# Weights of the node stages loaded one stage ahead, and the score weights of two layers made in the listing stage

## The chip, the cores and the metric

The kernel runs on 1 core of one Trainium2 chip. The metric is the device time of one execution in microseconds, the median of several runs.

## The reference

A graph with 3125 nodes of 256 features and 50000 edges passes through four parts, each followed by `x = layernorm(x + part(x))`. The first applies a long product of plane rotations. The second, with which this change has to do most, is a gated network of three attention layers:

```
x0 = x * gate(x, query);  h = concat(x0, query, x * query)
h = relu(rgat(h, W1, q1, k1, b1))            # 4 heads of 128
h = h + relu(rgat(h, W2, q2, k2, b2))        # 4 heads of 128
h = relu(rgat(h, W3, q3, k3, b3))            # 1 head of 128
out = h @ proj_w + proj_b + x0, divided by its norm

def rgat(x, W, Q, K, b):                     # per edge type r
    xw = einsum('ni,rio->rno', x, W)
    alpha = softmax over the edges into dst of leaky_relu(xw[type, dst] @ Q + xw[type, src] @ K)
    return segment_sum(xw[type, src] * alpha, dst) + b
```

The third part gathers `h1[src]` times a filter of the edge features (two small layers), sums by dst and applies two output layers `o1`, `o2`. The fourth gathers `x @ W + b` by dst, takes the mean by src and is added. Everything is float32.

## The kernel before

The program is written out in `build` (L3099) as a row of stages. Each is one block in which every engine has its own stream, with semaphores between them, and at its end all engines meet at a barrier (`Mem.__exit__`, L87). Nothing of a stage starts before that. The nodes are cut into 25 tiles of 125.

- `layer0_list` (L112), the listing stage, lists the rotations of the first part. VectorE ranks the edges and makes six planes; TensorE turns a row with the windows of the chunks (L347), then the planes (L353, 24 turnings, two PSUM banks in turn); ScalarE copies them out (L333); VectorE goes on when all six are copied (L265). SP loads six inputs at the start (L158, L160), which VectorE waits for (L171).
- `attention` (L1235), phases sum1, sum2, sum3, sums over the edges of a layer. 424 steps of 125 edges go in 36 blocks of T = 12 steps. GpSimd gathers a row per edge and step (L1299) into a ring of three blocks, and waits for TensorE's sums only when the ring is full. SP loads a mask for each block when the one three blocks back is used (L1322 to L1325). VectorE makes the scores of a block once its 12 gathers have landed (L1492), TensorE sums (L1412), VectorE adds to the table `agg`.
- `nodes_attend` (L2041), phases attend1 and attend2, makes the table of the next layer out of `agg`. VectorE divides and adds the bias (`attend`), TensorE turns the tile (`turn`, L2109), ScalarE copies it (`take_turned`), TensorE multiplies it by the next layer's weights W (`table`, L2122, L2125) and by the score weights (L2130), VectorE and ScalarE copy the results out and SP stores them. In attend2 ScalarE first folds the rows kept from layer 1 (L2172), three tiles ahead. GpSimd scatters two or three columns of the source list and one of the queries per tile (L1206, L1213).
- The score weights are products of W with the key and query vectors q and k. They let a node's scores come out of the same multiplication as its table row. `projection_load` (L1689) loads q, k, W and the transposed W at the start of the node stage, TensorE forms the products (`score_weights`, L1698: 4 blocks x 2 edge types x 4 or 1 matmuls) ahead of the first table, and VectorE copies them (L1711). The same helper serves the gate stage, where nothing changes.
- `nodes_mix` (L2243) and `nodes_filter` (L2728) are the node stages after sum3 and after the filter sum. Each loads its weights at its start on SP, then its x rows by groups of four tiles, one group after the other; TensorE and VectorE wait for all the weights (`landed`). In `nodes_mix` VectorE adds the projection bias to the x rows (`outer_bias`, L2422) before it squares the first group.
- `filter_sum` (L2490) sums the filtered messages in 106 quads of four steps; SP loads edge features and selections ahead (L2559, L2565).

Matmuls and turnings in float32 are recorded as two instructions each, so 32 matmuls show as 64. A stage's order on each engine is the order in which its function issues; nothing rearranges it.

## Time and profile before

| | us |
|---|---|
| median of 3 runs | 5727.86 |
| lowest and highest | 5724.3, 5733.14 |
| the profiled execution | 5721.64 |
| its span | 5719.8 |
| TensorE busy in it | 3820.1 (67%) |
| GpSimd busy | 3434.1 (60%) |
| VectorE busy | 2961.3 (52%) |
| ScalarE busy | 1971.7 (34%) |

The span runs from the first to the last recorded instruction. No engine is busy throughout: the stages have different limits, and a share over the whole span says little about one of them. The mean granted clock of TensorE is 0.772 of full speed; it has two levels, 1.2 and 2.4 GHz, shown as 0.50 and 1.00. In the rows PE is TensorE's matmuls, PEld its weight loads, DVE VectorE, ACT ScalarE, POOL GpSimd, SP the engine that issues most transfers; a q behind the name (SPq) marks the issue itself.

### The profile page before, as it was taken

To read this page: it belongs to the slowest core of one execution; us is meant where nothing else is said; L and a number is where in the kernel's file an instruction comes from. 1 tells how busy PE (TensorE), PEld (TensorE's weight loads), DVE (VectorE), ACT (ScalarE), POOL (GpSimd) and SP (SyncE) were. 2 spreads that over 40 slices of the span, in tenths; PEclk is the share of its full clock that TensorE was granted. 3 is DMA by queue.
4 is the path that set the end of the run, shared out by engine and by line. 5 is a ranking of instruction groups with operands and counts; after the bars stand their busy time and mean duration, and the time that the engine had idled before them with its cause. 6 is when DMAs were issued, how large, how long until landed. Compare 5 with 4: busy or idle time off the path is not lost. (4 is left out here: it accounts for less than half of the span.)

```text
span 5719.8 us, 76686 instructions
## 1 busy us (share of the span) xinstructions
PE 3820.1 (67%) x19501; PEld 2762.5 (48%) x19509; DVE 2961.3 (52%) x6738; ACT 1971.7 (34%) x4763; POOL 3434.1 (60%) x2759
## 2 busy tenths in 40 slices
PE   6599721795777769677776534444499998655553
PEld 6466510453555555355555433333367776433332
DVE  6666547422555542355554444444477887433334
ACT  0133200001666641266565112121089998200000
POOL 0122220377887735677773788885677776488884
PEclk6699955797888889788888755555799999766565
DMA  0000012234666633566663333332355554343332
GB/s 8 19 13 13 11 35 79 73 76 103 175 176 165 167 101 90 127 176 170 159 163 86 69 80 84 85 83 81 78 144 149 150 148 129 78 104 84 84 84 72
DMA packets 536302, 567.65 MB, mean 99 GB/s; under 512 B 327551, under 2 KB 419741, under 8 KB 535915
## 3 DMA queue, kind: packets, MB, share of 16 engines
q0 software_dynamic: 349600, 362.07, 26.4%
q1 hardware_dynamic: 183190, 196.56, 12.1%
q10 hardware_dynamic: 3250, 6.40, 0.4%
q14 instruction: 204, 1.67, 0.1%
q8 instruction: 58, 0.95, 0.1%
HBM read 469.70 MB, written 92.22 MB: 98 GB/s over the span
## 5 line engine op out<-in xcount | busy, mean ns | idle before, releaser
L1299 POOL DMA_INDIRECT sum_gx_sb<-scratch_xw,keep_k_row_step_sb x1272 | 1588.4, 1249 | 427.9 <-issue 355.2
L1412 PE MATMUL sum_a_ps<-sum_gx_sb,sum_sel_sb 125*125 125x258 f32 (+1 forms) x4320 | 1190.1, 438 | 459.5 <-ACT sum_gx_sb L1348 178.9
L1412 PEld LDWEIGHTS sum_a_ps<-sum_gx_sb,sum_sel_sb 125*125 125x125 f32 x4320 | 916.9, 238 | 647.4 <-issue 451.7
L1348 ACT ACTIVATE sum_gx_sb<-sum_gx_sb,sum_wt_sb 125x129 f32<-125x129 f32 x3312 | 981.8, 388 | 544.1 <-DVE sum_wt_sb L1541 544.1
L1206 POOL DMA_INDIRECT scratch_grouped<-keep_k_value_sb,keep_k_place_sb x400 | 481.1, 1203 | 252.6 <-issue 135.1
L2537 POOL DMA_INDIRECT filter_gx_sb<-scratch_h,keep_k_src_step_sb x424 | 529.0, 1248 | 170.7 <-issue 97.8
L3013 POOL DMA_INDIRECT source_gx_sb<-scratch_h,source_grouped_sb x424 | 526.6, 1242 | 140.2 <-issue 117.5
L3025 PE MATMUL source_s_ps<-source_gx_sb,source_sel_sb 125*125 125x257 f32 x848 | 371.1, 614 | 308.9 <-DMA source_gx_sb<-scratch_h,source_grouped_sb 308.9
L3025 PEld LDWEIGHTS source_s_ps<-source_gx_sb,source_sel_sb 125*125 125x125 f32 x848 | 246.8, 305 | 433.2 <-issue 172.4
L2599 PE MATMUL filter_ps<-filter_m_sb,filter_h_sb 128*125 128x256 f32 x1696 | 387.3, 381 | 8.0 <-DVE filter_h_sb L2669 7.4
L3053 DVE TENSOR_TENSOR keep_agg_sb<-source_s_ps,keep_agg_sb 125x257 f32 x424 | 181.1, 427 | 386.6 <-PE source_s_ps L3025 380.6
L2599 PEld LDWEIGHTS filter_ps<-filter_m_sb,filter_h_sb 128*125 128x125 f32 x1696 | 318.0, 188 | 64.9 <-DVE filter_h_sb L2669 17.2
L542 POOL TENSOR_TENSOR turn_lm_sb<-turn_lt_sb,turn_masks_sb 128x256 f32<-128x256 f32 x23 | 16.7, 725 | 551.8 <-DVEq L476 551.8
L1572 DVE TENSOR_TENSOR keep_agg_sb<-sum_a_ps,keep_agg_sb 125x516 f32 (+1 forms) x360 | 201.2, 559 | 150.4 <-PE sum_a_ps L1412 104.8
L3037 ACT ACTIVATE source_root_sb<-source_root_sb 125x25 f32<-125x25 f32 x1 | 0.2, 226 | 690.7 <-DVE source_root_sb L3089 690.7
L1548 DVE TENSOR_TENSOR sum_sel_sb<-sum_iota_sb,keep_k_dloc_sb 125x500 f32<-125x500 f32 x324 | 219.5, 678 | 36.2 <-issue 29.3
L2642 ACT ACTIVATE filter_lg_sb<-filter_lg_sb,filter_half_sb 128x1000 f32<-128x1000 f32 x212 | 230.0, 1131 | 7.4
L2639 ACT ACTIVATE filter_lg_sb<-filter_lg_sb 125x1024 f32<-125x1024 f32 (+1 forms) x212 | 210.6, 1040 | 7.3
L1341 ACT ACTIVATE sum_wexp_sb<-sum_dw_sb 48x126 f32<-48x126 f32 (+1 forms) x108 | 33.1, 307 | 499.7 <-DVEq L1531 499.6
L1580 DVE SCALAR_TENSOR_TENSOR keep_agg_sb<-keep_agg_sb,sum_fac_sb,sum_a_ps 125x129 f32 x324 | 93.5, 345 | 196.3 <-PE sum_a_ps L1412 189.1
L2675 DVE TENSOR_TENSOR filter_f_sb<-filter_ps,filter_mb_sb 125x1024 f32<-125x1024 f32 x106 | 129.8, 1225 | 123.8 <-PE filter_ps L2599 119.2
L2611 PE MATMUL filter_ps<-filter_ms_sb,filter_sel_sb 125*125 125x256 f32 x720 | 180.7, 394 | 6.2 <-issue 6.2
(520 smaller groups left out, 6342.3 us busy)
## 6 DMA issues: line engine op xcount, KB each, us to landing
scratch_hots<-sum_cuts_sb SPq DMA_DIRECT2D x108, 244.1 KB
filter_sel_sb<-scratch_hots SPq DMA_DIRECT2D x106, 244.1 KB
filter_ea_sb<-in_ea_t SPq DMA_DIRECT2D x848, 24.4 KB
sum_gx_sb<-scratch_xw,keep_k_row_step_sb POOLq DMA_INDIRECT x1272
scratch_xw<-gate_xsb_sb SPq DMA_DIRECT2D x50, 253.9 KB
scratch_xw<-attend_xsb_sb SPq DMA_DIRECT2D x25, 507.8 KB
filter_gx_sb<-scratch_h,keep_k_src_step_sb POOLq DMA_INDIRECT x424
source_gx_sb<-scratch_h,source_grouped_sb POOLq DMA_INDIRECT x424
```

The costliest lines, as they stand in the source:

```text
L1206: nc.gpsimd.indirect_dma_start(out=dr["grouped"], out_offset=bass.IndirectOffsetOnAxis(ap=keep["place"][:, t:t + 1], axis=0), in_=keep["va ...
L1299: nc.gpsimd.indirect_dma_start(out=gx[:, q, j, :], out_offset=None, in_=table, in_offset=bass.IndirectOffsetOnAxis(ap=keep["row_step"][:, ...
L1348: last = nc.scalar.activation(here, here, ACT.Copy, scale=wt[q][:, h, j:j + 1])
L1412: last = mm(psa[b][0:P, half, 0:BF], sel[:, 0, p, j, :], gx[:, q, at, half * BF:(half + 1) * BF], **flags)
L1548: vec.tensor_tensor(sel[:, 0, p], iota[0:P, 0:P].unsqueeze(1).broadcast_to([P, HF, P]), keep["dloc"][:, bass.ds(s * T + p * HF, HF)].unsqu ...
L1572: vec.tensor_tensor(here, psa[b][0:P, :, 0:BF], here, ALU.add).then_inc(added, steps)
L2537: nc.gpsimd.indirect_dma_start(out=gx[:, n % LAP, j, :], out_offset=None, in_=dr["h2"], in_offset=bass.IndirectOffsetOnAxis(ap=keep["src_s ...
L2599: last = mm(ps2[0:P, j, :], h1[r % 2][:, b, j * P:j * P + P], m2[:, b, :], start=(b == 0), stop=(b == 1))
L2639: nc.scalar.activation(lg[:], lg[:], ACT.Exp, scale=-1.0)
L2642: nc.scalar.activation(lg[:], lg[:], ACT.Ln, scale=0.5, bias=half[0:lg.shape[0], :]).then_inc(made, 1)
L3013: nc.gpsimd.indirect_dma_start(out=gx[:, h % RING, j, :], out_offset=None, in_=dr["h3"], in_offset=bass.IndirectOffsetOnAxis(ap=grouped[:, ...
L3025: nc.tensor.matmul(pss[q % 2][0:P, j, 0:W], sel[:, q % 2, j, :], gx[:, q, j, :], start=True, stop=True).then_inc(summed, 1)
```

## The change

- Layers 2 and 3: the score weights are made in the listing stage, from transposed weights and q, k vectors loaded there (2 x 1024 KB and 2 x 256 KB and the vectors) behind the stage's six first loads. TensorE makes them between the turning of the windows and that of the planes, ScalarE copies them (`keep_wk_sb`) after its two sines. They stay in SBUF.
- W of layers 2 and 3 is loaded during the sum stage before (`coming_w_sb`): SP's mask loop is cut in two, 3 rounds of 3 blocks, then the loads, then the rest. The six loads of `nodes_mix` go to the same place in sum3.
- The seven loads of `nodes_filter` are issued at the end of SP's laps in `filter_sum`.
- The four node stages no longer load weights, no longer wait for them, and form no score weights. The sum stages end only when the loads have landed.

The buffers of the weights live over two stages (`coming1` to `coming4`), which adds no barrier. The core of the diff:

```diff
+    psk = mem.ps("k")
+    later = [score_buffers(mem, 2, wk[0], 4, psk[:, 0:256]), score_buffers(mem, 3, wk[1], 1, psk[:, 256:512])]
...
+            for n, sc in zip((2, 3), later):
+                score_load(nc, sp, sc, dr[f"W{n}_t"], dr[f"L1_gnn_k{n}"], dr[f"L1_gnn_q{n}"], weights_in)
...
+            act.wait_ge(scores, 1)
+            for sc in later:
+                n = sc["blocks"] * 2 * 2 * sc["heads"]
+                nc.scalar.copy(sc["wk"][:].rearrange("p b r s -> p (b r s)"), sc["psk"][:, 0:n]).then_inc(scores_kept, 1)
+            act.wait_ge(scores_kept, 2)
...
             nc.tensor.transpose(psm[0:1, 8:8 + EP], first[:], ident[0:EP, 0:EP]).then_inc(win_made, 1)
+            pe.wait_ge(weights_in, 16 * 8)
+            for sc in later:
+                last = score_weights(nc, sc)
+            last.then_inc(scores, 1)
             pe.wait_ge(plane_made, 1)
...
-            with sp.Fori(0, NS // 3 - 1) as i:
+            def next_masks(i):
                 for q in range(3):
                     sp.wait_ge(mask_used, 3 * i + q + 1)
                     sp.dma_start(mk[:, q, :], dr["masks"][bass.ds(3 * i + q + 3, 1), 0:HT, :].rearrange(
                         "o p c -> p (o c)")).then_inc(m_in[q], 16)
                     if H == 1:
                         store_cuts(3 * i + q)
+
+            EARLY = 3
+            with sp.Fori(0, EARLY) as i:
+                next_masks(i)
+            if H == 4:
+                for r in range(2):
+                    sp.dma_start(coming[:, :, r, :], dr[f"L1_gnn_W{layer + 1}"][r].rearrange("(b p) o -> p b o", p=128)).then_inc(coming_in, 16)
+            else:
+                load_mix_weights(sp, dr, coming, coming_in)
+            with sp.Fori(EARLY, NS // 3 - 1) as i:
+                next_masks(i)
+            sp.wait_ge(coming_in, 16 * (2 if H == 4 else 6))
             if H == 1:
                 for s in range(NS - 3, NS):
...
+def score_buffers(mem, n, wk, heads, psk):
+
+    outs = {4: 4, 1: 1}[heads]
+    return dict(blocks=4, heads=heads, outs=outs, wk=wk, psk=psk, wt=mem.sb(f"wt{n}", [128, outs, 2, 512]),
+                qk=mem.sb(f"qk{n}", [128, outs, 2, heads]))
+
+
+def score_load(nc, sp, sc, wt, k, q, sem):
+    with nc.allow_non_contiguous_dma(reason="short rows of the key and query vectors"):
+        sp.dma_start(sc["qk"][:, :, 0, :], k.rearrange("(o p) h -> p o h", p=128)).then_inc(sem, 16)
+        sp.dma_start(sc["qk"][:, :, 1, :], q.rearrange("(o p) h -> p o h", p=128)).then_inc(sem, 16)
+    for r in range(2):
+        sp.dma_start(sc["wt"][:, :, r, :], wt[r].rearrange("(o p) b -> p o b", p=128)).then_inc(sem, 16)
 
...
-    pr = projection_buffers(mem, 4, F, H)
+    pr = dict(w=w, wk=wk, heads=H, width=F, psx=[mem.ps(f"x{r}") for r in range(2)], psk=mem.ps("k"))
...
-            projection_load(nc, sp, pr, *(dr[n] for n in names), weights_in)
...
-                if not t:
-                    pe.wait_ge(wk_made, 1)
...
-            pe.wait_ge(weights_in, 16 * PROJECTION_LOADS)
-            score_weights(nc, pr).then_inc(scores_made, 1)
...
-                    act.wait_ge(wk_made, 1)
...
-            dve.wait_ge(scores_made, 1)
-            take_score_weights(nc, pr)
-            dve.drain()
-            dve.nop().then_inc(wk_made, 1)
...
+def load_mix_weights(sp, dr, w, sem):
+    sp.dma_start(w["b3"][:], dr["L1_gnn_b3"].partition_broadcast(P)).then_inc(sem, 16)
+    sp.dma_start(w["ident"][:], dr["c_ident"]).then_inc(sem, 16)
+    sp.dma_start(w["pw"][:], dr["L1_gnn_proj_w"]).then_inc(sem, 16)
+    for n, name in (("pb", "L1_gnn_proj_b"), ("ab", "L2_gnn_aw_b")):
+        sp.dma_start(w[n][:], dr[name].partition_broadcast(P)).then_inc(sem, 16)
+    sp.dma_start(w["aw"][:], dr["L2_gnn_aw_W"].rearrange("(b p) o -> p b o", p=128)).then_inc(sem, 16)
+
...
-            sp.dma_start(b3[:], dr["L1_gnn_b3"].partition_broadcast(P)).then_inc(landed, 16)
-            sp.dma_start(ident[:], dr["c_ident"]).then_inc(landed, 16)
-            sp.dma_start(pw[:], dr["L1_gnn_proj_w"]).then_inc(landed, 16)
-            for t, name in ((pb, "L1_gnn_proj_b"), (ab, "L2_gnn_aw_b")):
-                sp.dma_start(t[:], dr[name].partition_broadcast(P)).then_inc(landed, 16)
-            sp.dma_start(aw[:], dr["L2_gnn_aw_W"].rearrange("(b p) o -> p b o", p=128)).then_inc(landed, 16)
...
-            pe.wait_ge(landed, 16 * 6)
...
-            dve.wait_ge(landed, 16 * 6)
...
+def load_filtered_weights(nc, sp, dr, w, sem):
+    with nc.allow_non_contiguous_dma(reason="a short vector"):
+        sp.dma_start(w["b1"][:], dr["L2_gnn_o1_b"].rearrange("(b p) -> p b", p=128)).then_inc(sem, 16)
+    sp.dma_start(w["ident"][:], dr["c_ident"]).then_inc(sem, 16)
+    for n, name in (("w1", "L2_gnn_o1_W"), ("w2", "L2_gnn_o2_W"), ("w3", "L3_gnn_W")):
+        sp.dma_start(w[n][:], dr[name].rearrange("(b p) o -> p b o", p=128)).then_inc(sem, 16)
+    for n, name in (("b2", "L2_gnn_o2_b"), ("b3", "L3_gnn_b")):
+        sp.dma_start(w[n][:], dr[name].partition_broadcast(P)).then_inc(sem, 16)
...
             laps(sp, lap)
+            load_filtered_weights(nc, sp, dr, coming, coming_in)
+            sp.wait_ge(coming_in, 16 * 7)
...
-            pe.wait_ge(landed, 16 * 7)
...
-            act.wait_ge(landed, 16 * 7)
...
-            dve.wait_ge(landed, 16 * 7)
...
+        for n, width, heads in ((1, 512, 4), (2, 128, 1)):
+            with phase(f"coming{n}") as held:
+                w = held.sb("w", [128, 4, 2, width])
+                with phase(f"sum{n}") as mem:
+                    attention(nc, mem, dr, keep, agg, 4, 512, n, w)
+                with phase(f"attend{n}") as mem:
+                    nodes_attend(nc, mem, dr, keep, agg, f"L1_gnn_b{n}", w, wk[n - 1], width, heads, n == 1)
+        with phase("coming3") as held:
+            weights = mix_weights(held)
+            with phase("sum3") as mem:
+                attention(nc, mem, dr, keep, agg, 1, 128, 3, weights)
+            with phase("mix") as mem:
+                nodes_mix(nc, mem, dr, keep, agg, weights)
+        with phase("coming4") as held:
+            weights = filtered_weights(held)
+            with phase("filter") as mem:
+                filter_sum(nc, mem, dr, keep, agg, weights)
+            with phase("filtered") as mem:
+                nodes_filter(nc, mem, dr, keep, agg, weights)
```

TensorE in the listing stage, from its first matmuls on. `listed_m_ps` gets the small products and the turned windows (the third row), `listed_t_ps` the planes. Before:

```order
L344 MATMUL listed_m_ps<-listed_rank_sb,listed_tri_sb 125x1
L345 MATMUL listed_m_ps<-listed_rank_sb,listed_ones_sb 125x1
L347 MATMUL listed_m_ps<-listed_ident_sb,listed_first_sb 1x125
L353 MATMUL listed_t_ps<-listed_ident_sb,listed_planes_sb 100x125 x24
L364 MATMUL listed_c_ps<-listed_valued_sb,listed_picked_sb 64x32 x500
```

and now:

```order
L354 MATMUL listed_m_ps<-listed_rank_sb,listed_tri_sb 125x1
L355 MATMUL listed_m_ps<-listed_rank_sb,listed_ones_sb 125x1
L357 MATMUL listed_m_ps<-listed_ident_sb,listed_first_sb 1x125
L1747 MATMUL listed_k_ps<-listed_qk_sb,listed_wt_sb 128x8 x32
L1747 MATMUL listed_k_ps<-listed_qk_sb,listed_wt_sb 128x2 x8
L367 MATMUL listed_t_ps<-listed_ident_sb,listed_planes_sb 100x125 x24
```

Forty score matmuls (`listed_k_ps`) stand ahead of the planes.

TensorE at the head of attend1, from the turning of tiles 0 and 1 on (`attend_t_ps`); `attend_x_ps` is the table, `attend_k_ps` the scores. Before:

```order
L2109 MATMUL attend_t_ps<-attend_ident_sb,attend_raw_sb 128x125 x8
L1705 MATMUL attend_k_ps<-attend_qk_sb,attend_wt_sb 128x8 x32
L2122 MATMUL attend_x_ps<-attend_w_sb,attend_ht_sb 125x512 x8
L2130 MATMUL attend_k_ps<-attend_wk_sb,attend_ht_sb 125x16 x4
L2109 MATMUL attend_t_ps<-attend_ident_sb,attend_raw_sb 128x125 x4
```

and now:

```order
L2150 MATMUL attend_t_ps<-attend_ident_sb,attend_raw_sb 128x125 x8
L2163 MATMUL attend_x_ps<-coming_w_sb,attend_ht_sb 125x512 x8
L2169 MATMUL attend_k_ps<-keep_wk_sb,attend_ht_sb 125x16 x4
L2150 MATMUL attend_t_ps<-attend_ident_sb,attend_raw_sb 128x125 x4
L2163 MATMUL attend_x0b_ps<-coming_w_sb,attend_ht_sb 125x512 x4
```

The first table follows the turning at once.

SP's order in sum2, now: the masks of the first rounds, the two loads, the masks of the rest (before, one loop of masks stood there).

```order
L1340 DMA sum_mk_sb<-scratch_masks 48x501
L1346 REGISTER_ALU
L1346 COMPARE_AND_BRANCH
L1350 DMA coming_w_sb<-in_L_gnn_W 128x4x128 x2
L1353 UNCONDITIONAL_BRANCH
L1353 ISA
L1340 ISA
L1340 DMA sum_mk_sb<-scratch_masks 48x501
```

The loads stand behind the waits for nine used masks. In sum1 it is the same with 128x4x512.

## Rows read from the trace of the kernel before

**Rows 1.** Busy time by stage, windows: stretch, its length, busy us (x instructions) of PE, PEld, DVE, ACT, POOL; clock, DMA share, GB/s.

```profile
1378.00:2108.00 730.00, 535.56 (x2192) 402.93 (x2192) 399.76 (x1145) 448.23 (x1482) 532.02 (x428) 0.84 0.61 160
2110.00:2366.00 256.00, 220.96 (x764) 121.82 (x764) 52.72 (x178) 26.83 (x50) 120.22 (x100) 0.90 0.40 96
2366.00:3112.00 746.00, 545.32 (x2192) 408.70 (x2192) 399.95 (x1145) 446.61 (x1481) 531.21 (x428) 0.83 0.60 156
```

**Rows 2.** Timeline, head of attend1: start, us, engine, line, out<-in, shapes, xcount [idle before <-releaser].

```profile
2115.36 2.05 PE L2109 MATMUL attend_t_ps<-attend_ident_sb,attend_raw_sb 125*128 125x125 f32 x8 [7.92 <-DVE attend_raw_sb L2198]
...
2130.08 13.82 PE L1705 MATMUL attend_k_ps<-attend_qk_sb,attend_wt_sb 128*128 128x8 f32 x64 [12.67 <-DMA attend_wt_sb<-in_W_t]
...
2143.76 9.90 PE L2122 MATMUL attend_x_ps<-attend_w_sb,attend_ht_sb 128*125 128x512 f32 x16
```

**Rows 3.** Windows in attend1, and one timeline row of small matmuls at full clock.

```profile
2110.00:2130.00 20.00, 2.05 (x8) 1.41 (x8) 6.49 (x14) 1.18 (x2) 3.60 (x3) 0.55 0.75 253
2130.00:2144.00 14.00, 13.92 (x65) 13.92 (x66) 0.06 (x1) 0.00 (x0) 0.00 (x0) 0.50 0.00 1
...
2153.00:2347.00 194.00, 194.00 (x668) 101.56 (x667) 44.03 (x156) 25.07 (x47) 114.33 (x96) 1.00 0.42 96
...
2153.49 0.94 PE L2130 MATMUL attend_k_ps<-attend_wk_sb,attend_ht_sb 128*125 128x16 f32 x8
```

**Rows 4.** Timeline, head of the listing stage.

```profile
9.38 0.37 DVE L172 CAST listed_fi_sb<-listed_r_src_sb 125x400 f32<-125x400 int32 x1 [4.22 <-DMA listed_iota_sb<-in_c_iota]
...
28.90 0.37 PE L347 MATMUL listed_m_ps<-listed_ident_sb,listed_first_sb 125*1 125x125 f32 x1 [6.24 <-DVEq L248]
...
33.13 1.91 PE L353 MATMUL listed_t_ps<-listed_ident_sb,listed_planes_sb 125*100 125x125 f32 x8 [3.87 <-DVEq L261]
...
40.25 0.99 DVE L270 TENSOR_TENSOR listed_inchunk_sb<-listed_tp_sb,listed_iota_sb 100x800 f32<-100x800 f32 x1 [6.81 <-ACT listed_tp_sb L333]
```

**Rows 5.** Timeline, head and end of attend2.

```profile
3126.28 1.05 ACT L2150 ACTIVATE attend_ht_sb<-attend_t_ps 128x500 f32<-128x500 f32 x2
...
3130.85 3.58 PE L1705 MATMUL attend_k_ps<-attend_qk_sb,attend_wt_sb 128*128 128x2 f32 x16 [5.37 <-DMA attend_wt_sb<-in_W_t]
3134.29 3.76 PE L2125 MATMUL attend_x_ps<-attend_w_sb,attend_ht_sb 128*125 128x256 f32 x8
...
3140.44 1.20 POOL L1213 DMA_INDIRECT scratch_qe<-attend_qsb_sb,keep_k_q_row_sb  x1 [24.18 <-DVEq L2221]
...
3252.27 1.18 POOL L1213 DMA_INDIRECT scratch_qe<-attend_qsb_sb,keep_k_q_row_sb  x1 [0.30 <-issue]
```

**Rows 6.** Timeline, head of the mix stage.

```profile
3967.15 0.28 SPq L2276 DMA_DIRECT2D mix_b_sb<-in_L_gnn_b  x1
...
3969.55 0.38 SPq L2285 DMA_DIRECT2D mix_xa_sb<-scratch_x  x1
...
3975.84 2.19 DVE L2416 SCALAR_TENSOR_TENSOR mix_raw_sb<-keep_agg_sb,mix_den_sb,mix_b_sb 125x128 f32<-125x128 f32 x8 [7.57 <-DMA mix_aw_sb<-in_L_gnn_aw_W]
...
3985.25 1.22 DVE L2422 TENSOR_TENSOR mix_xa_sb<-mix_xa_sb,mix_pb_sb 125x1024 f32<-125x1024 f32 x1 [7.23 <-DMA mix_xb_sb<-scratch_x]
...
3996.70 1.23 DVE L2422 TENSOR_TENSOR mix_xa_sb<-mix_xa_sb,mix_pb_sb 125x1024 f32<-125x1024 f32 x1 [1.02 <-DMA mix_xb_sb<-scratch_x]
```

**Rows 7.** Timeline, end of the filter sum and head of the output stage.

```profile
4826.44 18.64 SPq L2565 DMA_DIRECT2D filter_sel_sb<-scratch_hots  x4
...
4855.90 0.42 DVE L2689 TENSOR_TENSOR keep_agg_sb<-filter_ps,keep_agg_sb 125x256 f32 x1 [2.82 <-PE filter_ps L2611]
4857.45 0.40 SPq L2761 DMA_DIRECT2D filtered_b_sb<-in_L_gnn_o_b  x1
...
4857.99 1.77 DVE L2901 MEMSET filtered_hs_sb<- 125x2056 f32 x1 [0.40 <-issue]
...
4867.07 1.93 PE L2801 MATMUL filtered_a_ps<-filtered_ident_sb,keep_agg_sb 125*128 125x125 f32 x8 [11.32 <-DMA filtered_b_sb<-in_L_gnn_b]
```

**Rows 8.** Waits in sum1 (who <- whom: us, times, longest), and a timeline row at its end.

```profile
DVE sum_sc_sb L1492 <- DMA sum_gx_sb<-scratch_xw,keep_k_row_step_sb: 36.4, 20, 4.4
...
2097.82 9.62 PE L1412 MATMUL sum_a_ps<-sum_gx_sb,sum_sel_sb 125*125 125x258 f32 x38
```

More of the change, by code:

```diff
@@ L109, with layer0_list @@
 SPLIT = 13
-def layer0_list(nc, mem, dr, col, turns):
+def layer0_list(nc, mem, dr, col, turns, wk):
     T100 = EF // SUBS
@@ L1232, in part_tiles, with attention @@
     return values
-def attention(nc, mem, dr, keep, agg, heads, width, layer):
+def attention(nc, mem, dr, keep, agg, heads, width, layer, coming):
     H, W = heads, width // heads
@@ L1286, in attention @@
     PARTS = T // HF
+    coming_in = nm("coming_in")
     with nc.Block() as block:
@@ L2054, in nodes_attend @@
     xsb, qsb = mem.sb("xsb", [P, RING, 2, FW + H]), mem.sb("qsb", [P, NT, 2, H])
-    (bias_in, ident_in, weights_in, scores_made, wk_made, raw_made, turned, ht_made, projected, rest_taken, taken, grouped, put,
+    (bias_in, ident_in, raw_made, turned, ht_made, projected, rest_taken, taken, grouped, put,
      q_out, kept_used) = (mem.sem(n) for n in (
-         "bias_in", "ident_in", "weights_in", "scores_made", "wk_made", "raw_made", "turned", "ht_made", "projected", "rest_taken",
+         "bias_in", "ident_in", "raw_made", "turned", "ht_made", "projected", "rest_taken",
          "taken", "grouped", "put", "q_out", "kept_used"))
@@ L2250, in nodes_mix @@
     raw, ht = mem.sb("raw", [P, 2, GN, 128]), mem.sb("ht", [128, 2, GN * P])
-    b3, ident = mem.sb("b3", [P, 128]), mem.sb("ident", [128, 128])
-    pb, ab, idle = mem.sb("pb", [P, D]), mem.sb("ab", [P, D]), mem.sb("idle", [128, 512], mybir.dt.bfloat16)
-    pw, aw = mem.sb("pw", [128, D]), mem.sb("aw", [128, 2, D])
+    b3, ident, pb, ab, pw, aw = (weights[n] for n in ("b3", "ident", "pb", "ab", "pw", "aw"))
+    idle = mem.sb("idle", [128, 512], mybir.dt.bfloat16)
     xa, xb = mem.sb("xa", [P, NT, D]), mem.sb("xb", [P, NT, D])
@@ L2725, in _, with nodes_filter @@
             laps(dve, lap)
-def nodes_filter(nc, mem, dr, keep, agg):
+def nodes_filter(nc, mem, dr, keep, agg, weights):
     LAST, GN = len(GROUPS) - 1, 4
@@ L2733, in nodes_filter @@
     stats, mv = mem.sb("stats", [P, NT, 6]), mem.sb("mv", [P, NT, 2])
-    w1, w2, w3 = (mem.sb(n, [128, 2, D]) for n in ("w1", "w2", "w3"))
-    b1, half = mem.sb("b1", [128, 2]), mem.sb("half", [128, 1])
-    b2, b3 = mem.sb("b2", [P, D]), mem.sb("b3", [P, D])
-    ident = mem.sb("ident", [128, 128])
+    w1, w2, w3, b1, b2, b3, ident = (weights[n] for n in ("w1", "w2", "w3", "b1", "b2", "b3", "ident"))
+    half = mem.sb("half", [128, 1])
     at, lg, f1, h1 = (mem.sb(n, [128, 2, GN * P]) for n in ("at", "lg", "f1", "h1"))
@@ L2759, in _ @@
         def _(sp):
-            with nc.allow_non_contiguous_dma(reason="a short vector"):
-                sp.dma_start(b1[:], dr["L2_gnn_o1_b"].rearrange("(b p) -> p b", p=128)).then_inc(landed, 16)
-            sp.dma_start(ident[:], dr["c_ident"]).then_inc(landed, 16)
-            for t, name in ((w1, "L2_gnn_o1_W"), (w2, "L2_gnn_o2_W"), (w3, "L3_gnn_W")):
-                sp.dma_start(t[:], dr[name].rearrange("(b p) o -> p b o", p=128)).then_inc(landed, 16)
-            for t, name in ((b2, "L2_gnn_o2_b"), (b3, "L3_gnn_b")):
-                sp.dma_start(t[:], dr[name].partition_broadcast(P)).then_inc(landed, 16)
             for g in range(LAST + 1):
@@ L3113, in build @@
         mt = keeper.sb("mt", [128, 2, D])
+        wk = [keeper.sb(f"wk{n}", [128, 4, 2, 2 * heads]) for n, heads in ((2, 4), (3, 1))]
         with phase("steps") as columns:
@@ L3117, in build @@
             with phase("listed") as mem:
-                layer0_list(nc, mem, dr, col, turns)
+                layer0_list(nc, mem, dr, col, turns, wk)
             with phase("turn") as mem:
```

38 lines of the change are left out of this document (15 added, 23 removed).

## The prediction

> **What bounds the kernel now.** The program is a row of stages with a barrier between each two, so a change is worth what it takes off the chain inside its stage. I read four views. First the busy times by stage: in the stage of the first node layer TensorE is busy for 220.96 of 256 us, and the two sums over 4 heads before them take 730 and 746 us for the same work [rows 1]. Then the instructions in order of time at the head of each stage that the change touches, to see what its first table waits for [rows 2, 5 to 7]. Then the windows around the score matmuls, for clock and rate [rows 3]. Last the head of the listing stage, where the score work goes [rows 4], and the waits of the first sum stage, where the weights go [rows 8].
>
> **Node layer 1: -26.3 us.** Before, TensorE turns tiles 0 and 1 until 2115.36 + 2.05 = 2117.41; ScalarE takes the first of them meanwhile. Then TensorE stands until the weights land at 2130.08, runs the 32 score matmuls (64 recorded instructions) for 13.8 us, and starts the first table at 2143.76 [rows 2]. Afterwards table 0 needs only the two turned tiles: 2117.4, so 2143.76 - 2117.41 = 26.3 us earlier. From there TensorE is never idle (194.00 busy in 194.00 us [rows 3]), and GpSimd's four transfers per tile, 1.49 us each [rows 5], fill 6.0 us of a tile that takes 8.2 (220.96 less the 2.05 and 13.82 us ahead of the tables, over 25 tiles), so the shift reaches the end of the stage. The clock is at its lower level, 0.50 to 0.55, from the stage's start up to the tables [rows 3], so it is low at 2117.4 too, and the slow start of the tables stays.
>
> **Node layer 2: -7.4 us.** Here the weights stand behind the first four transfers of rows kept from layer 1. ScalarE folds three of those first and takes the turned tiles at 3126.28 + about 0.55 for the first of two, 3126.9. The score matmuls run from 3130.85, the first table from 3134.29 [rows 5]. Without them it starts at 3126.9: 7.4 us. After the first table GpSimd sets the pace, from its first put at 3140.44 to its last at 3252.27, 75 instructions less the two already done, 1.49 us each, without a gap [rows 5]. Its start hangs on the first table, so the shift still goes through; what is late next is the kept rows, and those don't move.
>
> **Mix stage: -6.6 us.** VectorE waits for all six weight loads until 3975.84, but that wait isn't the one that counts: its next step waits for the first group of x rows, issued behind the weights, until 3985.25. The second group is issued at 3985.25 and used at 3996.70, so a group takes 11.4 us on its own [rows 6]. With the weights gone the first is issued when the stage opens, 3967.15, and is there at 3967.2 + 11.4 = 3978.6: 6.6 us earlier, not the 7.6 us that VectorE stood for the weights. The least it can be is the earlier issue alone, 3969.55 - 3967.15 = 2.4 us, if the weights ahead cost the x rows nothing; the most is the 7.6 us. I take the difference, since both of its ends are landings of the same kind.
>
> **Output stage of the filter: -7.2 us.** TensorE's first turning starts when the weights have landed, 4867.07. Its next condition is VectorE's fill, 4857.99 + 1.77 = 4859.8 [rows 7]. Difference 7.2 us. The x rows, 0.5 MB a group, are issued as the stage opens, and VectorE needs them 12 us later, longer than the 11.4 us of mix's pair of twice that size. The loads move to the end of the filter sum: SP issues its last selection at 4826.44 + 18.64 = 4845.1, and the loads landed 4867.07 - 4857.45 = 9.6 us after their first issue, so at 4854.7, before VectorE's last add at 4855.90. Cover left: 1.2 us; without it up to 2 us come back.
>
> **Listing stage: +13.4 us.** TensorE turns the windows at 28.90 + 0.37 = 29.27 and, before, turns the planes from 33.13 [rows 4]. Now 40 score matmuls stand between (32 with 8 columns, 8 with 2; 80 recorded instructions). Price of one: 13.82 / 64 = 0.216 us at clock 0.50; the same kind at clock 1.00 takes 0.94 / 8 = 0.118 us [rows 2, 3]. 80 x 0.216 = 17.3 us, so planes start at 29.3 + 17.3 = 46.6 instead of 33.13, 13.4 us late (at full clock 38.7, 5.6 us late). I take the slow value: the row for just this work shows the clock at 0.50 through all of it. ScalarE's two small copies lie beside the planes' turning. Nothing hides the delay, since VectorE's next large step at 40.25 waits for the six planes, and it stands idle for 6.8 us before it already [rows 4]. The 2.6 MB that these matmuls read are issued from about 3.3 us, behind the stage's six first loads; at the 253 GB/s of a window full of such loads [rows 3] they need 10.4 us and are there by some 14 us, ahead of 29.3. At half that rate they come at 24 us, still ahead. Those first loads, which VectorE waits for until 9.38, stand in front in the same queue: nothing for them, 3 us as the bound, a third of the 9.38.
>
> **Sum stages: +1 us.** 2.1 MB for layer 1 are issued after 9 of 36 blocks, 0.5 MB and 0.8 MB in the two later sums. They share the DMA engines with the gathers: bound 2.1 / 0.253 = 8.3 us, and nothing from below. VectorE's score step waited for gathers 20 times in this stage, 36.4 us in all, 4.4 us at most, and the buffers hold three blocks [rows 8]. A short lag is absorbed; I take 1 us. The Trainium skill (DMA: Bandwidth & Descriptors, section on queues, rings and completion order) has each engine take turns between its queues by packet. By that rule the gathers would get half of each engine while the weights pass, which would then take 16.6 us instead of 8.3, and with the gathers' share of 0.61 the lag would be some 16.6 x 0.11 / 0.61 = 3 us, an estimate; the sum would be 5697 us.
>
> **Sum.** -26.3 - 7.4 - 6.6 - 7.2 + 13.4 + 1 = -33.1 us. The profiled execution has 5721.64 us (span 5719.8), 6 us under the median 5727.86; taken from the median, since the differences don't depend on that, this is 5694.8, so **5695 us**.
>
> **Rivals.**
> The clock is high in the listing. For it: nothing in the listing's rows says how long TensorE stays slow, and the planes' turning there gets faster within the burst (8 in 1.91 us, against 8 in 2.05 at the head of layer 1). Against it: 13.9 us of the same matmuls at 0.50. Delay 5.6 instead of 13.4: 5687 us. Chance 0.05.
> The gathers pay. The 2 MB come while GpSimd runs without slack, busy for 532.02 of 730 us with a gap before each issue, and what they lose isn't made up: up to +8.3 instead of +1, 5702 us. For it: the 36.4 us of waits. Against: no wait longer than 4.4 us, and a gather is waited for in 20 blocks of 36 only [rows 8]. The rule on turns between queues, above, is a milder form of this. Chance 0.08.
> Starts don't count. The queue of GpSimd's scatters, not the first table or x rows, sets the ends of layer 2 and mix, and 14 us of gain vanish: 5709 us. For it: GpSimd without a gap in layer 2. Against it: that run starts only with the first put. Chance 0.07.
> The change doesn't do what it says: the loads, though issued earlier, are waited for at the end of their sum stages, so the gains vanish and only the listing's delay is left less the work moved out, near 5728 us. Against it: they are issued with 27 of 36 blocks to go. Chance 0.02.
> Slower: the clock falls in the first sum. A gather lag opens a gap on TensorE, the clock drops to 0.50 and stays there for blocks. A block's 48 recorded matmuls with 258 columns take 9.62 / 38 = 0.253 us each at the stage's end; at half clock twice that, 12 us more per block, of which about 5 us lie in TensorE's idle time (535.56 busy of 730): 7 us a block [rows 1, 8]. It cancels the gain from 5 blocks on, is slower by over 0.2% from 7 on, and 8 give +56 - 33: 5751 us. For it: mean clock 0.84, so it already drops at times. Against: it rises again each time. Chance 0.04.
>
> **How the numbers follow.** My forecast has 0.74. What a measurement can tell from no change is 0.2%, 11.5 us, so the border of faster is 5716.4. Forecast and the first three rivals lie below, 0.94 in all; I take 0.04 off, because two sum stages with the same work differ by 16 us [rows 1], and such a shift in both can eat the gain. Faster 0.90, same 0.06, slower 0.04. Range: low end 5681, the fast listing with 6 us for the sums' own variation; high end 5711, just past the rival in which starts don't count. That leaves out less than 2 in 10.
>
> **What would show it.** In the new profile: the table of layer 1 starts 7.6 us after its stage's first issue instead of 34; that of layer 2 some 14 us after instead of 21.6; VectorE's x step in mix 11.5 us after the stage opens instead of 18.1; the output stage turns 2.4 us after; the planes of the listing start at 46.6 with clock 0.50 before. Sum stages stay within 5 us of 730 and 746. A listing delay under 8 us, a first sum longer by over 8 us, or a stage whose first table comes early and whose end doesn't move would prove that step wrong.

## The result, and the profile after

The changed kernel took 5698.61 us in the median of 4 runs (5695.75 to 5699.24), the kernel before beside it 5729.37 (4 runs). Ratio 0.9946, 95% interval [0.9929, 0.9963]: 30.8 us or 0.54% faster. The forecast was 5695 us, 33.1 us less, with a range from 5681 to 5711.

Below, one of the twelve runs of the kernel with the score matmuls back in the node stages took 7931.14 us and is left out of its time and ratio.

First the stages. The windows of the changed kernel, each from the first instruction of a stage to that of the next (stretch, length, busy us of PE, PEld, DVE, ACT, POOL; clock, DMA share, GB/s): the listing, sum 1, node layer 1, sum 2, node layer 2, sum 3, mix, the output stage of the filter, and the last stage.

```profile
0.80:215.50 214.70, 132.41 (x1117) 129.96 (x1117) 135.65 (x219) 9.25 (x13) 0.00 (x0) 0.62 0.07 20
1391.70:2136.80 745.10, 543.14 (x2192) 408.81 (x2192) 399.83 (x1146) 448.18 (x1482) 535.49 (x428) 0.83 0.61 159
2136.80:2364.10 227.30, 205.05 (x700) 107.53 (x700) 52.74 (x178) 26.82 (x50) 120.39 (x100) 0.96 0.39 89
2364.10:3109.40 745.30, 540.32 (x2192) 406.82 (x2192) 399.90 (x1146) 446.68 (x1481) 533.34 (x428) 0.83 0.61 157
3109.40:3249.50 140.10, 92.58 (x500) 79.32 (x500) 61.56 (x203) 27.95 (x50) 91.78 (x75) 0.80 0.34 73
3249.50:3954.60 705.10, 288.39 (x1304) 235.81 (x1304) 317.97 (x1040) 142.65 (x470) 535.94 (x429) 0.51 0.33 82
3954.60:4117.20 162.60, 88.48 (x330) 57.95 (x337) 72.35 (x213) 10.20 (x15) 106.82 (x89) 0.76 0.31 80
4833.90:4965.70 131.80, 91.51 (x356) 65.12 (x356) 62.55 (x126) 33.75 (x37) 71.30 (x58) 0.83 0.30 74
4965.70:5697.40 731.70, 374.36 (x848) 248.14 (x848) 288.16 (x637) 1.45 (x2) 530.31 (x424) 0.58 0.35 85
```

Against [rows 1], node layer 1 falls from 256.0 to 227.3 us, and TensorE's busy time in it by 15.9: the 13.8 us of score matmuls are gone and the wait ahead of them too. Sum 1, though, is 745.1 us long where it was 732.4 in the profile of before (from its first instruction to that of the next stage, 2.4 us more than the window of [rows 1]), and the last stage, which the change doesn't touch, 731.7 where it was 723.5. The two profiles differ by 22.4 us in their spans, the medians of the runs by 30.8. These two stages are what the experiments had to explain.

The heads of the stages, from the timelines of the changed kernel. Node layer 1, against [rows 2]:

```profile
2136.66 0.28 SPq L2111 DMA_DIRECT2D attend_bb_sb<-in_L_gnn_b  x1
...
2142.43 2.06 PE L2150 MATMUL attend_t_ps<-attend_ident_sb,attend_raw_sb 125*128 125x125 f32 x8 [7.78 <-DVE attend_raw_sb L2234]
...
2144.28 7.87 PE L2163 MATMUL attend_x_ps<-coming_w_sb,attend_ht_sb 128*125 128x512 f32 x16
```

The table starts 7.6 us after the first issue (34 before) and runs 16 recorded matmuls in 7.87 us, not 9.90. Node layer 2, against [rows 5], and mix, against [rows 6]:

```profile
3109.26 0.28 SPq L2111 DMA_DIRECT2D attend_bb_sb<-in_L_gnn_b  x1
...
3122.90 3.78 PE L2166 MATMUL attend_x_ps<-coming_w_sb,attend_ht_sb 128*125 128x256 f32 x8 [0.51 <-ACT attend_ht_sb L2187]
...
3954.50 0.27 SPq L2324 DMA_DIRECT2D mix_xa_sb<-scratch_x  x1
...
3965.90 1.23 DVE L2459 TENSOR_TENSOR mix_xa_sb<-mix_xa_sb,coming_pb_sb 125x1024 f32<-125x1024 f32 x1 [8.01 <-DMA mix_xb_sb<-scratch_x]
```

Now 13.6 us (21.6) and 11.4 us (18.1). The output stage, against [rows 7], and the listing, against [rows 4]:

```profile
4832.22 0.42 DVE L2744 TENSOR_TENSOR keep_agg_sb<-filter_ps,keep_agg_sb 125x256 f32 x1 [2.47 <-PE filter_ps L2666]
...
4836.19 1.93 PE L2847 MATMUL filtered_a_ps<-coming_ident_sb,keep_agg_sb 125*128 125x125 f32 x8 [4.12 <-DVEq L2946]
...
28.83 0.37 PE L357 MATMUL listed_m_ps<-listed_ident_sb,listed_first_sb 125*1 125x125 f32 x1 [6.24 <-DVEq L253]
28.99 17.07 PE L1747 MATMUL listed_k_ps<-listed_qk_sb,listed_wt_sb 128*128 128x8 f32 x80
45.92 1.89 PE L367 MATMUL listed_t_ps<-listed_ident_sb,listed_planes_sb 125*100 125x125 f32 x8
```

The output stage turns 2.4 us after its start (4833.8). The 80 recorded score matmuls of the listing take 17.07 us, and the planes start 12.8 us later than before (45.92 against 33.13).

### The profile page after: what moved, and what is told of

Its sections match the earlier page's. It is cut to its first block and busy times, and to the rows that moved or that the text cites. A ratio compares the mean times of both kernels' runs of the same rounds, so it can differ in the third digit from the quotient of the medians.

```text
span 5697.4 us, 76686 instructions
## 1 busy us (share of the span) xinstructions
PE 3818.7 (67%) x19501; PEld 2765.9 (49%) x19509; DVE 2960.2 (52%) x6736; ACT 1972.0 (35%) x4765; POOL 3442.5 (60%) x2759
## 3 DMA queue, kind: packets, MB, share of 16 engines
q0 software_dynamic: 349600, 362.07, 26.6%
## 5 line engine op out<-in xcount | busy, mean ns | idle before, releaser
L3056 POOL DMA_INDIRECT source_gx_sb<-scratch_h,source_grouped_sb x424 | 530.3, 1251 | 140.1 <-issue 114.2
```

What stands on the lines that cost most here:

```text
L3056: nc.gpsimd.indirect_dma_start(out=gx[:, h % RING, j, :], out_offset=None, in_=dr["h3"], in_offset=bass.IndirectOffsetOnAxis(ap=grouped[:, ...
```

## The experiments

A profile is one execution, so two more profiles show how much a stage varies by itself; each time below is the median of 5 to 12 runs, and its ratio is to 17 or 25 runs of the kernel before on the same chip. Three chips were used, so ratios are compared and not times. A "meeting" is a load of weights that passes while the gathers run.

### The kernel before and the changed kernel once more

> The kernel before, once more, for the variation of its stages. Theory A: first sum 732 us within 2 us again, gathers issued over 669 us. Theory B: first sum 736 us or more, and the last stage (723.5 us in the first profile, 727 to 732 in all five later ones) longer too. Ratio 1 within 0.002.

> The changed kernel once more, on the same chip as the others of this series. Theory A: score step waits 8 us or more for gathers at block 10 of the first sum, gathers issued over 674-680 us, first sum 739-746 us. Time 5694-5700 us.

Before again: 5731.42 us, ratio 0.9999 [0.9990, 1.0008]. Changed again: 5704.80 us, ratio 0.9952 [0.9939, 0.9965]. The changed kernel is above the 5694 to 5700 us expected. The first row is the window of sum 1 in the kernel before, again; the waits rows are the score step's for gathers in this stage (who, for whom: us, times, longest), of the kernel before again and of the changed kernel again.

```profile
1381.80:2124.20 742.40, 540.34 (x2192) 406.52 (x2192) 400.34 (x1146) 448.39 (x1482) 537.24 (x428) 0.84 0.60 157
```

```profile
DVE sum_sc_sb L1492 <- DMA sum_gx_sb<-scratch_xw,keep_k_row_step_sb: 40.8, 19, 4.6
```

```profile
DVE sum_sc_sb L1519 <- DMA sum_gx_sb<-scratch_xw,keep_k_row_step_sb: 38.8, 17, 7.6
```

Sum 1 of the untouched kernel is 742.4 us here and was 732.4 in the first profile: theory B holds for most of the 12.7 us. The changed kernel repeats its 745.1 us, with 7.6 us as the longest wait, where theory A wanted 8 or more. The last stage is 724.1 us in the kernel before and 731.8 in the changed one, as in the first pair: that difference isn't the variation of one profile, and theory B's second half (a longer last stage too) fails.

### Weights later, and in pieces

```diff
+            with sp.Fori(0, NS // 3 - 1) as i:      # late, and behind the gathers
+                next_masks(i)
+            sp.wait_ge(mask_used, NS - 1)           # behind the gathers alone
...
+                for n in range(8):                  # in pieces
+                    next_masks(EARLY + n)
+                    b, r = n // 2, n % 2
+                    sp.dma_start(coming[:, b, r, :], dr[f"L1_gnn_W{layer + 1}"][r, b * 128:b * 128 + 128]).then_inc(coming_in, 16)
```

> The changed kernel, but the weights of the next stage are issued behind the last masks of each sum over the nodes, when nearly all gathers are done, instead of after 9 of 36 blocks. Theory A, the 2 MB of weights cost the first sum its 13 us, because they share the DMA engines with the gathers for some 10 us and the lag isn't made up: first sum back from 745 to 731-735 us, no wait of the score step for gathers over 5 us near block 10, time 5698.6 - 11 = about 5688 us. Theory B, the 13 us are the variation of this stage from run to run: first sum anywhere between 730 and 746, time within 3 us of 5698.6. Both expect the first table of node layer 1 still some 8 us after its stage's first issue.

> The changed kernel, but the weights of node layers 1 and 2 come in eight pieces (one block of 128 rows of one direction each, 256 KB in the first), one piece after every third block of the sum, instead of two transfers of 1 MB behind each other. Theory A, what costs is the length of the collision: a piece takes 1 us of the engines, less than what the three blocks of buffers hold, so the lag is absorbed each time: first sum 731-737 us, time 5687-5691 us. Theory A', what the gathers lose is their share of bytes however these are spread: first sum 740-745 us, time 5694-5699 us. Theory B (variation): 5698.6 within 3 us, whatever the sum shows.

> The changed kernel, but the weights of the next stage are issued once the weights of block 35 of 36 have been taken, so behind the last gather of each sum (the late variant before issued them 16 us ahead of the last gathers, and its score step then waited 6.9 us in one piece). Theory A (the collision with the gathers is what costs): the gathers are issued over 669 us as before the change, no wait of the score step near block 10 nor near block 34, first sum 731-734 us, profiled span 6 us under that of the changed kernel run beside it at least. Theory B (the first sum's length varies by itself): still 738 us or more. Both: weights landed some 10 us after issue, before the stage's end, so the table of node layer 1 starts 8 us after the first issue; if they land late, that table is late by the rest.

Measured: late 5700.44 us, ratio 0.9957 [0.9941, 0.9973], sum 1 739.7 us; in pieces 5692.14 us, 0.9946 [0.9930, 0.9962], 738.5 us; behind the gathers 5710.46 us, 0.9963 [0.9950, 0.9976], 745.2 us. The late loads were issued at 2052, 15 us ahead of the last gather, and the score step's longest wait, 6.9 us, stands there: the meeting had only moved. In pieces, no wait for gathers is over 3.9 us, but 738.5 us lies between the two ranges of theory A and theory A' and decides nothing, and the ratio is the changed kernel's. The loads behind the gathers meet none, as the waits show, and the sum is no shorter:

```profile
1399.10:2144.30 745.20, 548.38 (x2192) 411.27 (x2192) 399.98 (x1146) 448.33 (x1482) 535.51 (x428) 0.83 0.61 159
```

```profile
DVE sum_sc_sb L1517 <- DMA sum_gx_sb<-scratch_xw,keep_k_row_step_sb: 38.4, 18, 4.0
```

No wait is over 4.0 us, against 10.7 in the changed kernel, and theory A's 731 to 734 us fall. The edit had a fault of its own: in sum 3, which stores its selections through SP, the stores of the last blocks stood behind the new wait, and that sum took 718.2 us instead of 705.

### The same weights four times

```diff
+                for n in range(4):
+                    if n:
+                        next_masks(EARLY + n - 1)
+                        sp.wait_ge(coming_in, 16 * 2 * n)
                     for r in range(2):
```

> The changed kernel, but the weights of node layers 1 and 2 are loaded four times over into the same buffer, each time after three more blocks of the sum (the loads after the first are useless work). So the gathers of the first sum meet 2 MB four times instead of once. Theory A (each meeting costs the gathers 4 to 5 us that stay): first sum 757-762 us instead of 745, time +13 to +17. Theory B (the wait at block 10 is real but is worked off later, and the first sum's length varies by itself between 732 and 746): first sum 743-749 us, waits of up to 10 us after each load, time within 5 us of the changed kernel.

```profile
1394.90:2154.50 759.60, 541.97 (x2192) 406.94 (x2192) 400.21 (x1146) 448.25 (x1482) 536.16 (x428) 0.82 0.65 164
```

```profile
DVE sum_sc_sb L1526 <- DMA sum_gx_sb<-scratch_xw,keep_k_row_step_sb: 50.8, 16, 9.8
```

5714.46 us, ratio 0.9979 [0.9969, 0.9989], sum 1 759.6 us, in theory A's range. Three more meetings cost 759.6 - 742.7 = 17 us, 5.6 each, where 742.7 is the mean of the six profiles with one meeting at this place (739.0 to 745.1); the ratios say 15 to 19 us. The issue of the gathers steps back at these loads: 4.1, 1.8 and about 10 us at blocks 15, 18 and 21, against the variant with the mix loads put back. So a meeting does cost, and the cost stays.

A single one is no larger than what the whole stage varies by. The six profiles without a meeting there (732.4, 742.5, 739.0, 739.7, 745.2, 745.8) have a mean of 740.8: 1.9 us less than with it, within their spread. At the place itself it is clear. From the first gather of block 11 to that of block 12 GpSimd takes 20.8 to 22.2 us in the seven profiles with a load there and 18.4 to 19.0 in the seven without, 2.8 us more in the mean. The gathers' own durations don't grow; what is added is one wait for TensorE to free a buffer, here in the changed kernel (window 1590:1640) and then at the fourth load of this variant (window 1775:1830), with VectorE's wait just before:

```profile
POOL sum_gx_sb L1314 <- PE sum_a_ps L1439: 4.8, 4, 3.9
```

```profile
POOL sum_gx_sb L1314 <- PE sum_a_ps L1446: 13.3, 3, 11.8
DVE sum_both_sb L1534 <- issue: 9.3, 3, 8.8
```

Of the 11.8 us at the fourth load a part isn't the gathers': VectorE stood 8.8 us ahead of its scan of a block after that block's gathers and the weights had landed, a wait that is 3.7 to 4.5 us in the other 13 profiles. Why it was longer is open. One meeting thus puts the gathers back by 2.8 us where it happens; for the stage's length the figures are 1.9 us (not clear of nothing) to 5.6 us.

### The score matmuls in TensorE's idle time

```diff
+            pe.wait_ge(weights_in, 16 * 8)
+            score_weights(nc, later[1]).then_inc(scores, 1)   # layer 3, ahead of the windows
             pe.wait_ge(wins, 1)
...
                 last.then_inc(turned, 1)
+            score_weights(nc, later[0]).then_inc(scores, 1)   # layer 2, behind the planes
             for b in range(NBATCH):
```

> The changed kernel, but in the listing stage TensorE makes the score weights of layer 3 (16 recorded matmuls, 3.5 us) while it waits for the windows, and those of layer 2 (64 recorded, 13.8 us at clock 0.50) after the turning of the planes, while VectorE prepares the first batch; ScalarE copies both after the planes. Theory: the listing is late by 12.8 us only because the matmuls stand ahead of the planes on TensorE: planes turned from about 33.5 us, listing stage ends 11-13 us earlier, time about 5686-5687 us. Rival: the 2.6 MB that the listing loads, or the longer busy TensorE, cost by themselves: the stage gains less than 6 us, time over 5692 us. Second rival: the layer 2 matmuls take longer than TensorE's idle time of 14.7 us before the first batch and push this batch back by 1 to 4 us: 5688-5691 us.

```profile
22.36 3.55 PE L1746 MATMUL listed_k_ps<-listed_qk_sb,listed_wt_sb 128*128 128x2 f32 x16
28.74 0.37 PE L359 MATMUL listed_m_ps<-listed_ident_sb,listed_first_sb 125*1 125x125 f32 x1 [2.82 <-DVEq L253]
32.97 1.91 PE L365 MATMUL listed_t_ps<-listed_ident_sb,listed_planes_sb 125*100 125x125 f32 x8 [3.87 <-DVEq L266]
...
39.00 10.68 PE L1746 MATMUL listed_k_ps<-listed_qk_sb,listed_wt_sb 128*128 128x8 f32 x64
53.95 2.34 PE L377 MATMUL listed_c_ps<-listed_valued_sb,listed_picked_sb 100*64 100x32 f32 x20 [4.26 <-DVE listed_valued_sb L281]
```

5684.90 us, ratio 0.9923 [0.9910, 0.9935]. Planes turn at 32.97, the first batch waits for VectorE's picks and not for the scores (4.26 us idle ahead of it), and the listing is back at 202.2 us, with the 2.6 MB still loaded in it; without them it is 201.9, in the variant with the score weights back in the node stages. So the delay was the place of the matmuls on TensorE.

With the weights behind the gathers as well:

> The weights behind the gathers, and in the listing stage the score matmuls of layer 3 ahead of the windows, those of layer 2 behind the planes' turning. Theory: both savings stand side by side, listing 12.5 us less than the changed kernel, first sum 10-12 us less: 5674-5678 us, ratio to the kernel before 0.990-0.992. If only the listing's saving is real: 5685 us.

5697.66 us, ratio 0.9946 [0.9932, 0.9959]: sum 1 745.8 us, and sum 3 714.6 us, by the same fault as above. The forecast of 5674 to 5678 us failed with theory A, on which it stood.

### The score weights back in the node stages

The edit is the change undone there: the transposed weights are loaded at the stage's head and `score_weights` stands ahead of `table(0)` again, while `coming` is kept.

> The changed kernel without the move of the score weights: they are made in the node stages again, from transposed weights loaded there; the projection weights still come one stage ahead. Listing -12.8 us. Node layer 1: 2 MB instead of 4 MB to load, landed some 8 us sooner than before the change (about 13 us after the stage's first issue), then 13.8 us of matmuls, first table about 27 us after the first issue instead of 7.6: +19 us. Node layer 2: +4 us (3.5 us of matmuls behind a short load). Sum +10 us, about 5709 us, if starts of the tables count as forecast. Rival (starts don't count, GpSimd's queue sets the ends): -12.8 + 0 to 5 us, 5686-5691 us.

```profile
2129.38 2.05 PE L2140 MATMUL attend_t_ps<-attend_ident_sb,attend_raw_sb 125*128 125x125 f32 x8 [8.02 <-DVE attend_raw_sb L2229]
2135.32 13.82 PE L1733 MATMUL attend_k_ps<-attend_qk_sb,attend_wt_sb 128*128 128x8 f32 x64 [3.88 <-DMA attend_wt_sb<-in_W_t]
```

5713.23 us, ratio 0.9975 [0.9965, 0.9985], above the 5709 expected. Layer 1 takes 246.9 us, 19.4 more than with the change (+19 expected), layer 2 145.7, 6.2 more (+4 expected), the listing 13 less. Of layer 1's gain some two thirds come from the score weights and one third from the earlier projection weights.

### The mix loads back

`load_mix_weights` is issued at the head of `nodes_mix` again, with its waits.

> The changed kernel, but the six weight loads of the mix stage are issued at the head of that stage again, ahead of the x rows. Mix stage so far 161-164 us in eight profiles with the change and 172.9 and 170.1 in the two of the kernel before. Theory (the loads delay the x rows by 6.6 us and the rest of the stage follows): mix 170-173 us, the x step of VectorE 18 us after the stage opens, time +7 to +9 us. Rival (part of the gain in mix came from elsewhere): mix 166-168 us. The third sum, without these loads in it, stays at 705-709 us.

```profile
3961.45 2.19 DVE L2455 SCALAR_TENSOR_TENSOR mix_raw_sb<-keep_agg_sb,mix_den_sb,coming_b_sb 125x128 f32<-125x128 f32 x8 [6.68 <-DMA coming_aw_sb<-in_L_gnn_aw_W]
...
3970.43 1.23 DVE L2461 TENSOR_TENSOR mix_xa_sb<-mix_xa_sb,coming_pb_sb 125x1024 f32<-125x1024 f32 x1 [6.79 <-DMA mix_xb_sb<-scratch_x]
```

5702.80 us, ratio 0.9961 [0.9948, 0.9974]. The x step comes 16.8 us after the stage opens (3953.7), 5.4 later than with the change, and the stage is 168.4 us, 5.3 over its mean of 163.1: the shift of the x rows passes through to the end. That is nearer to the rival's 166 to 168 us than to the theory's 170 to 173; the time is 5 to 9 us over the changed kernel by the ratios. Of the 8.7 us that mix gained, the loads explain 5.3, and 3.4 stay open (its three profiles of before spread over 2.8).

### The place of the buffers

The score weights that stay in SBUF take 4 x 2 x (8 + 2) x 4 = 320 bytes per partition, and they are held ahead of all other buffers of the later stages.

```diff
         mt = keeper.sb("mt", [128, 2, D])
+        keeper.sb("pad", [128, 80])     # the kernel before, 320 bytes
+        keeper.sb("pad", [128, 48])     # with the listing's new order, 192 bytes more
```

> The kernel before with 320 bytes per partition held from the start and never used, as the changed kernel holds 320 bytes for the score weights, so that all later buffers of the last stage lie 320 bytes further on, where the changed kernel has them. It computes the same. Theory S (the last stage is longer after the change because its buffers lie elsewhere): from the last gather to the end 67 us instead of 63, last stage 728-732 us instead of 723.5 and 724.1, time 4 to 8 us over the kernel before, ratio 1.001. Rival (it is something else that the change did, such as its code or the order of the stages before): 63 us, 723-725 us, ratio 1.000.

> The kernel with the score matmuls moved within the listing stage (5684.9 us before), and 192 unused bytes more, so that the output buffer lies 512 bytes further on than in the kernel before instead of 320. Theory S with a place that repeats every 512 bytes: last gather to end 63 us, last stage 724 us, time 4 to 8 us lower than without the 192 bytes, 5677-5681 us on the same kind of chip. If the place doesn't repeat like that or doesn't matter: 67 us and 5685 us. Listing stage 202 us in either case.

The stores of the output at the end of the program: windows of 21 us in their midst and of what is left up to the end (the last figure is GB/s). First the kernel before, then the same shifted by 320 bytes, then the changed kernel, then the variant with 512 bytes in all.

```profile
5695.00:5716.00 21.00, 0.00 (x0) 0.00 (x0) 2.11 (x7) 0.00 (x0) 0.00 (x0) 0.50 0.34 121
5716.00:5719.80 3.80, 0.00 (x0) 0.00 (x0) 0.00 (x0) 0.00 (x0) 0.00 (x0) 0.50 0.22 77
```

```profile
5704.00:5725.00 21.00, 0.00 (x0) 0.00 (x0) 0.00 (x0) 0.00 (x0) 0.00 (x0) 0.50 0.33 112
5725.00:5731.70 6.70, 0.00 (x0) 0.00 (x0) 0.00 (x0) 0.00 (x0) 0.00 (x0) 0.50 0.12 41
```

```profile
5667.00:5688.00 21.00, 0.00 (x0) 0.00 (x0) 2.61 (x9) 0.00 (x0) 0.00 (x0) 0.50 0.33 110
5688.00:5697.40 9.40, 0.00 (x0) 0.00 (x0) 0.00 (x0) 0.00 (x0) 0.00 (x0) 0.50 0.18 63
```

```profile
5649.00:5670.00 21.00, 0.00 (x0) 0.00 (x0) 2.60 (x9) 0.00 (x0) 0.00 (x0) 0.50 0.34 121
5670.00:5674.30 4.30, 0.00 (x0) 0.00 (x0) 0.00 (x0) 0.00 (x0) 0.00 (x0) 0.50 0.23 82
```

Shifted by 320 bytes, the kernel before shows the changed kernel's last stage: stores at 112 instead of 121 GB/s, 67.6 us from the last gather to the end instead of 62.9 and 63.1, and 729.9 us for the stage. With 512 bytes it is 62.5 and 723.0 us. For the stage's length theory S holds, and so in all ten profiles of changed kernels with 320 bytes (66.6 to 67.7 us, stage 727.2 to 731.8). From the first store to the end it is 29.1 to 29.2 us in the three profiles with 0 or 512 bytes and 33.7 to 34.3 in the eleven with 320. The times don't show it: shifted 5727.76 us, ratio 1.0007 [0.9997, 1.0017], which holds both 1.0000 and the 1.001 expected; with 512 bytes 5681.44 us, ratio 0.9920 [0.9905, 0.9935], some 2 us under the same order without the 192 bytes (0.9923) where 4 to 8 were expected. It is the lowest ratio of all versions, 0.26% below the changed kernel (0.9946), and nearly all of that is the listing's new order.

## Why the prediction was right, step by step

Profiles of before and of the changed stages, by their means (3 profiles of before, 2 for the last stage; 6 to 11 that leave the stage as the change has it):

| step | forecast | measured |
|---|---|---|
| node layer 1 | -26.3 | 256.2 to 227.5: -28.7 |
| node layer 2 | -7.4 | 147.7 to 139.5: -8.2 |
| mix | -6.6 | 171.8 to 163.1: -8.7 |
| output stage of the filter | -7.2 | 138.4 to 131.5: -6.9 |
| listing | +13.4 | 202.1 to 215.1: +13.0 |
| sums | +1 | +4.7, +0.8, -3.4; filter sum +0.2 |
| last stage | 0 | 723.8 to 729.7: +5.9 |
| other stages | 0 | +2.0 |
| sum | -33.1 | -29.3 |

The medians of the runs gave -30.8. That the total came so near is partly luck: the four node stages gave 52.5 us instead of 47.5, and what no step had, in the last stage and the others, took 7.9 us back.

**Node layer 1.** The start moved by 26.6 us (34.3 to 7.6 after the first issue) and reached the end, since TensorE stays busy. The other 2.1 us contradict one clause, that "the slow start of the tables stays". These windows are 10 us from the first table on, the kernel before, then the changed one:

```profile
2143.80:2153.80 10.00, 10.00 (x21) 4.41 (x21) 1.37 (x5) 0.00 (x0) 0.00 (x0) 0.72 0.00 0
```

```profile
2144.30:2154.30 10.00, 10.00 (x32) 5.15 (x32) 2.28 (x10) 1.45 (x3) 0.17 (x1) 0.92 0.16 53
```

Behind 14 us of score matmuls at a clock of 0.50 (the lower level, 1.2 GHz) the first tables ran 21 matmuls in 10 us; straight behind the turnings they run 32, at 0.92, and the first 16 recorded table matmuls take 7.87 us instead of 9.90.

**Node layer 2 and the output stage** came as worked out, start and end. Its cover held too: the filter's loads began at 4821.76, SP leaves its wait for them at 4831.6, and the last add is at 4832.22: 0.6 us of cover, not 1.2, and 718.2 us for that sum against 718.0.

**Mix** moved by the x rows and not by VectorE's wait for the weights, as forecast: 6.7 us by the change, 5.4 by putting the loads back. The stage itself gained 8.7, and 3.4 of that are open, as said.

**Listing.** The size was right: the price was 17.07 / 80 = 0.213 us where the forecast took 0.216. Its sign, "clock 0.50 before", can't be checked. The row shows 1.00 (2.4 GHz):

```profile
29.30:46.20 16.90, 16.90 (x81) 16.90 (x82) 3.73 (x7) 0.10 (x1) 0.00 (x0) 1.00 0.00 1
```

But the first clock entry in this trace is at 50.1 us, and the view shows 1.00 where there is no entry. The kernel before shows this in two profiles of the same stretch, the first with entries from 36.5 us on, the second with none before 232:

```profile
50.00:100.00 50.00, 46.34 (x435) 46.34 (x435) 35.52 (x36) 0.00 (x0) 0.00 (x0) 0.50 0.01 1
```

```profile
50.00:100.00 50.00, 46.15 (x433) 46.15 (x434) 35.66 (x36) 0.00 (x0) 0.00 (x0) 1.00 0.01 1
```

The same work takes the same time, once at 0.50 and once at a 1.00 that nobody measured. (For the same reason the 0.62 of the listing's row in the first table is too high.) In the variant with the score matmuls in TensorE's idle time the entries begin at 38.9 us, just ahead of the 64 matmuls of 8 columns. Its windows before and after the clock's fall:

```profile
39.00:42.20 3.20, 3.20 (x32) 3.20 (x30) 1.68 (x2) 1.42 (x2) 0.00 (x0) 1.00 0.00 0
42.40:49.50 7.10, 7.10 (x35) 7.10 (x34) 7.03 (x2) 0.00 (x0) 0.00 (x0) 0.50 0.01 2
```

In its trace they start every 0.111 us in the first and every 0.214 us in the second. So 0.213 us is the price of the lower level, and the rival of the fast clock didn't come true.

**Sums.** The mis-sized term: 1 us stands for 2.8 us at the meeting in sum 1. "A short lag is absorbed" is half right: the score step's wait at block 10 is 6.9 to 10.7 us in the profiles with the load and at most 2.5 without, and the buffers take up most of it; the 2.8 us that reach GpSimd's issue aren't made up, as four loads showed. The rival's +8.3 was not reached by one meeting. The prediction's own sign, a first sum longer by over 8 us, did show in the first pair of profiles; but the untouched kernel's second profile is 10 us longer too, so the sign was finer than the stage's own variation. The Trainium skill (DMA: Bandwidth & Descriptors, section on queues, rings and completion order), whose rule on turns gave an estimate of 3 us, fits the 2.8 us in size; that turns between queues are the cause no run here shows. The rival that the clock falls in sum 1 didn't happen (mean 0.83 after, 0.84 before). The 4.7 us of the table are mostly the low first profile of before. That sum 3 was 3.4 us shorter in the mean is not explained.

**What no step had** is the last stage: 5.9 us for 320 bytes. Without it the sum of the steps would have been -35.2 us, against the forecast's -33.1.

## What to carry to other kernels

Loads that open a stage are worth moving as far as the instruction that waited for them has nothing else to wait for; read that next condition from the timeline, and carry work into an earlier stage only where the engine is idle there: the same matmuls cost 13 us ahead of the planes and nothing behind them. Before a stage's length in two profiles is put down to a change, take the untouched kernel's profile again: up to 10 of 12.7 us were its own variation. Where a small cost drowns in that, look at the place where it arises: 2.8 us were clear in the issue of twelve gathers and lost in a stage of 740 us. A clock column is worth a second look where the same work takes the same time at two values of it. And a few bytes kept for the whole program move every later buffer; a stage whose code is the same and whose time isn't is a reason to look at addresses.

## What the runs showed of the hardware

- Stores of 625 KB from 125 partitions ran at 121 GB/s with the buffers where the kernel before has them and 512 bytes further, and at 110 to 112 GB/s 320 bytes further, in the windows shown. The last stage's gathers took 1242 to 1243 ns in the mean in the three profiles with 0 or 512 bytes and 1241 to 1251 with 320, so they don't tell the two apart. What about the place matters wasn't tried.
- The score matmuls of 8 columns took 0.216 us each at a clock of 0.50 in node layer 1, and in one burst of the listing 0.111 us at 1.00 and 0.214 at 0.50: their price follows the clock. A clock of 1.00 ahead of a trace's first clock entry (at 36.5 to 52.1 us in seven of the profiles, at 231.6 to 245.6 in the other seven) is no measurement.
- 2 MB that meet a stream of gathers without slack put its issue back by 2.8 us in the mean of seven profiles. Three more of them in one profile put it back by 1.8 to 10 us each, though the load was the same, and it stayed back: 17.2 us at block 21, 18.7 at block 34, against the variant with the mix loads put back.
